# Cross-attention on one core: the first head's weights in two halves, xT behind pair 1's weights, and seven small warm-up matmuls on zeros from VectorE

## What is computed

```python
Q = (x @ Wq).reshape(B, -1, H, D).transpose(0, 2, 1, 3)
K = (ctx @ Wk).reshape(B, -1, H, D).transpose(0, 2, 1, 3)
V = (ctx @ Wv).reshape(B, -1, H, D).transpose(0, 2, 1, 3)
score = jnp.einsum('bhqd,bhkd->bhqk', Q, K) / math.sqrt(D)
attn = softmax(where(mask, score, -inf))
out = einsum('bhqk,bhkd->bqhd', attn, V).reshape(B, -1, H * D) @ Wo + x
return (out - mean) * rsqrt(var + 1e-5) * gamma + beta
```

## Time and profile before

| | |
|---|---|
| median of 3 runs | 318.01 us (317.92 to 318.31) |
| profiled execution, own time | 317.95 us |
| profiled execution, span from first to last instruction | 316.1 us |
| outside the span | 1.85 us |
| TensorE busy | 309.5 us (98%) |
| granted TensorE clock over the span | 0.997 |

### The profile page before, as it was taken

How to read it: one execution, slowest core, us unless ns; L and a number is a source line. 1 busy time by engine, 2 the same in 40 slices (tenths; PEclk the granted TensorE clock), 3 DMA queues, 4 the chain that set the end, 5 groups by cost and what they waited for, 6 DMA issues and landing times.

```text
span 316.1 us, 8051 instructions
## 1 busy us (share of the span) xinstructions
PE 309.5 (98%) x2584; PEld 303.4 (96%) x2584; DVE 253.1 (80%) x721; ACT 222.0 (70%) x601; POOL 181.3 (57%) x183
## 2 busy tenths in 40 slices
PE   8999999999999999999999999999999999999993
PEld 7998889999999999999999999999999999999992
DVE  0467778777999789987998889987998889975686
ACT  2446677768867787678777797678767887777640
POOL 1123476457864587558855586558755686457212
PEclk9999999999999999999999999999999999999998
DMA  7996443564354454384446535364355435440101
GB/s 254 358 400 242 137 150 117 158 218 134 98 163 160 159 175 140 141 239 142 133 126 208 172 133 163 129 214 156 113 187 185 170 100 184 143 155 4 35 0 66
DMA packets 46911, 50.27 MB, mean 159 GB/s; under 512 B 3504, under 2 KB 37040, under 8 KB 46896
## 3 DMA queue, kind: packets, MB, share of 16 engines
q1 hardware_dynamic: 46608, 49.56, 47.0%
q10 hardware_dynamic: 288, 0.52, 0.7%
HBM read 32.24 MB, written 17.83 MB: 158 GB/s over the span
## 4 chain that ended last, share of the span: by engine, by line
PE 95%; DMA 2%; DVE 1%; SPq 1%; POOLq 0%; issue 0%; POOL 0%
PE score_bank L321 25%; PE out_bank L321 19%; PE gL_bank L321 14%; PE tL_bank L321 13%; PE tU_bank L321 9%; PE gU_bank L321 7%; DMA wq_raw<-in_wqT 2%; PE spare_bank L321 1%; PE tL_bank L355 1%; PE spare_bank L355 1%; PE tL_bank L337 1%; PE tU_bank L337 1%; PE out_bank L361 1%; PE tU_bank L361 1%; PE out_bank L337 0%; PE spare_bank L337 0%
## 5 line engine op out<-in xcount | busy, mean ns | idle before, releaser
L1017 POOL TENSOR_TENSOR probs<-probs,inv_sum 128x512 f32<-128x512 f32 x64 | 66.7, 1043 | 84.4 <-DVE inv_sum L804 83.8
L615 ACT ACTIVATE probs<-neg_scores,neg_max 128x256 f32<-128x256 f32 x128 | 64.1, 502 | 36.1 <-DVE neg_max L793 36.0
L1040 POOL TENSOR_TENSOR pT_lo<-pT_raw,pT_hi 128x512 fp32r<-128x512 f32 x60 | 76.6, 1297 | 8.6 <-ACT pT_hi L572 8.6
L793 DVE CUSTOM_DVE_ANT_0 neg_scores<-score_bank,mask_bias 128x256 f32<-128x256 f32 x128 | 49.1, 420 | 6.3 <-PE score_bank L321 3.9
L814 DVE STREAM_TRANSPOSE squares<-probs 128x512 f32<-128x512 f32 x60 | 42.3, 706 | 1.0 <-DMA scratch<-squares 0.8
L572 ACT ACTIVATE tL_hi<-tL_bank 128x512 fp32r<-128x512 f32 x31 | 18.6, 599 | 29.6 <-PE tL_bank L321 29.6
L321 PE MATMUL score_bank<-ctxT_hi,gU 128*128 128x256 f32 x128 | 36.1, 282 | 0.0
L321 PE MATMUL score_bank<-ctxT_hi,gL_lo 128*128 128x256 f32 x128 | 35.9, 281 | 0.0
L321 PE MATMUL score_bank<-ctxT_lo,gU 128*128 128x256 f32 x128 | 35.9, 281 | 0.0
L321 PE MATMUL score_bank<-ctxT_lo,gL_hi 128*128 128x256 f32 x128 | 35.9, 280 | 0.0
L321 PE MATMUL score_bank<-ctxT_hi,gL_hi 128*128 128x256 f32 x128 | 35.6, 278 | 0.0
(11 more groups left out here) (167 smaller groups left out, 981.0 us busy)
## 6 DMA issues: line engine op xcount, KB each, us to landing
scratch<-squares SPq DMA_DIRECT2D x30, 512.0 KB, 2.8
pT_raw<-scratch SPq DMA_DIRECT2D x120, 128.0 KB, 3.1
xT_raw<-in_xT SPq DMA_DIRECT2D x8, 256.0 KB, 4.5
ctxT_raw<-in_ctxT SPq DMA_DIRECT2D x8, 256.0 KB, 4.7
wo_raw<-in_wo SPq DMA_DIRECT2D x4, 512.0 KB, 14.3
x_res<-in_x SPq DMA_DIRECT2D x8, 256.0 KB, 3.2
out<-y_out SPq DMA_DIRECT2D x7, 256.0 KB, 2.6
wq_raw<-in_wqT SPq DMA_DIRECT2D x3, 512.0 KB, 7.6
```

What stands on the lines that cost most here:

```text
L615: nc.scalar.activation(probs[j % 2][:, n, :], neg_scores[:, n, :], ACT.Exp, bias=neg_max[:, n:n + 1], scale=-1.0, accum_out=row_sum[:, n:n ...
L793: nc.vector.tensor_tensor_reduce(out=neg_scores[:, n, :], in0=score_bank[hh][:, q, :], in1=mask_bias[:], scale=-SCALE, scalar=3.0e38, op0= ...
L1017: nc.gpsimd.tensor_tensor(probs[j % 2][:, rows, :], probs[j % 2][:, rows, :], inv, ALU.mult) \
L1040: nc.gpsimd.tensor_tensor(pT_lo[j % 2][:, k].rearrange("p hh (q i r) -> p (hh q) i r", q=QT, i=ROWS), pT_raw[j % 2][:, k].rearrange("p i n ...
```

## The change

It has four parts. Head 0's wk and wq are loaded as one transfer per tile `d` instead of one per head, each with a semaphore of its own (`q_head_in[0]` and `[1]`; head 1 now has `q_head_in[2]`). `fold_A` runs `d` outside and `i` inside, for all heads, and waits for each `d` of head 0 apart. SyncE issues xT behind wk and wq of pair 1. The warm-up is 7 matmuls of 128 columns instead of 4 of 256, on zeros that VectorE sets (128x128) instead of GpSimd (128x256).

```diff
-WARMING = 4
+WARMING = 7
-        zeros = sb("zeros", [P, DI])
+        zeros = sb("zeros", [P, P])
-        q_head_in = [sem(f"q_head_in{h}") for h in range(2)]
+        q_head_in = [sem(f"q_head_in{n}") for n in range(DT + 1)]
@@ sync
-            for j in range(PAIRS):
-                if j > 0:
-                    tiles = slice(2 * j * DT, 2 * (j + 1) * DT)
-                    sp.dma_start(wk_raw[:, tiles], wkT[:, tiles]).then_inc(q_weights_in[j], 16)
-                    sp.dma_start(wq_raw[:, tiles], wqT[:, tiles]).then_inc(q_weights_in[j], 16)
-                else:
-                    for h in range(2):
-                        tiles = slice(h * DT, (h + 1) * DT)
-                        sp.dma_start(wk_raw[:, tiles], wkT[:, tiles]).then_inc(q_head_in[h], 16)
+            for d in range(DT):
+                sp.dma_start(wk_raw[:, d:d + 1], wkT[:, d:d + 1]).then_inc(q_head_in[d], 16)
+            sp.dma_start(wk_raw[:, DT:2 * DT], wkT[:, DT:2 * DT]).then_inc(q_head_in[DT], 16)
+            for j in range(1, PAIRS):
+                tiles = slice(2 * j * DT, 2 * (j + 1) * DT)
+                sp.dma_start(wk_raw[:, tiles], wkT[:, tiles]).then_inc(q_weights_in[j], 16)
+                sp.dma_start(wq_raw[:, tiles], wqT[:, tiles]).then_inc(q_weights_in[j], 16)
+                if j == 1:
                     load_xT(0)
@@ tensor, fold_A
-                if h < 2:
-                    pe.wait_ge(q_head_in[h], 32)
-                elif h % 2 == 0:
+                if h == 1:
+                    pe.wait_ge(q_head_in[DT], 32)
+                elif h > 0 and h % 2 == 0:
                     pe.wait_ge(q_weights_in[h // 2], 32)
-                for i in range(IT):
-                    for d in range(DT):
+                for d in range(DT):
+                    if h == 0:
+
+                        pe.wait_ge(q_head_in[d], 32)
+                    for i in range(IT):
                         ins = nc.tensor.matmul(dst[:, i * DL:(i + 1) * DL],
                                                wq_raw[:, h * DT + d, i * P:(i + 1) * P],
-                                               wk_raw[:, h * DT + d, :], start=d == 0, stop=d == DT - 1)
+                                               wk_raw[:, h * DT + d, :], start=d == 0 and i == 0, stop=d == DT - 1,
+                                               skip_group_check=True)
@@ tensor
-                nc.tensor.matmul(score_bank[0][:, 0, :], zeros[:, 0:P], zeros[:], start=True, stop=True)
+                nc.tensor.matmul(score_bank[0][:, 0, 0:P], zeros[:], zeros[:], start=True, stop=True)
@@ scalar
-            for h in range(2):
-                tiles = slice(h * DT, (h + 1) * DT)
-                act.dma_start(wq_raw[:, tiles], wqT[:, tiles]).then_inc(q_head_in[h], 16)
+            for d in range(DT):
+                act.dma_start(wq_raw[:, d:d + 1], wqT[:, d:d + 1]).then_inc(q_head_in[d], 16)
+            act.dma_start(wq_raw[:, DT:2 * DT], wqT[:, DT:2 * DT]).then_inc(q_head_in[DT], 16)
@@ vector
+            nc.vector.memset(zeros[:], 0.0).then_inc(zeros_made, 1)
@@ gpsimd
-            nc.gpsimd.memset(zeros[:], 0.0).then_inc(zeros_made, 1)
```

## The result

| | before | after |
|---|---|---|
| median of 7 runs each | 317.94 us (317.92 to 318.31) | 319.10 us (318.57 to 319.50) |
| profiled execution, own time | 317.95 us | 319.14 us |
| its span | 316.1 us | 317.3 us |

The ratio is 1.0032, 95% interval 1.0022 to 1.0041: slower by 0.7 to 1.3 us, outside the predicted range (317.4 to 318.4). So the sign holds both times and the size is between 0.3 and 1.3 us. The ratios compare all runs of two kernels and not their medians alone, so the two can differ by some tenths of a microsecond.

A forecast was written before the change was run, and what follows sets the result against it. The prediction took the landing of pair 1's weights at 9.07 us, then unbroken TensorE work, as the bound. Moving xT (-0.34 us) plus the halves' cost (+0.25) gave -0.09 on 317.95: 317.9 us, range 317.4 to 318.4.

The forecast's parts named there:

- What bounds the start: Kernel start: pair 1's weights landing at 9.07 us set it, and TensorE follows in one piece.
- Nothing behind absorbs a shift: After the start: TensorE is busy 98% of the span, so the end moves as much as the folds.
- xT behind pair 1: Start's load stream: pair 1 lands 0.65 us earlier, but a wait at head 4 limits the gain to 0.34 us.
- o: Start's load stream: total delay from splitting head 0's loads, taken as 0.25 us, bounds 0 and 1.34.
- The halves start TensorE earlier, which is worth nothing: Head 0: TensorE starts 0.7 us earlier, at 4.0 us, but then waits for pair 1 anyway; no gain.
- packet time: Head 0's loads: 256 more packets at 9 ns fixed time each, over 16 engines, cost 0.15 us.
- two more completions: Head 0's loads: two more transfers, each with 16 completion writes at 9 ns, cost 0.02 us.
- the ramp: Stream up to 2.5 us: if half-size packets take as long there, 0.085 us is lost.
- the 12.1 that I had named as a sign of being wrong: Pair 2's wq, expected at 11.4 to 11.8 us: landing after 12.1 would show the prediction wrong.
- Slower, by the halves in the stream: First 3 us: packet rate, not bytes, limits the loads; sum toward +1.0 us, 318.9 us; chance 0.08.
- Slower, by the clock: TensorE at the start: array stays longer at its lower clock level, head 4 0.5 us late, 318.5 us; chance 0.07.
- Small packets are free: Head 0's loads: splitting costs only 0 to 0.05 us, so -0.3 us, 317.6 us; chance 0.2.

The follow-up runs named there:

- e5: Changed kernel with head 0's first tile alone and the other three tiles of heads 0 and 1 in one transfer, on both queues: 317.86 us, ratio 1.0002.
- e8: Kernel before with xT issued behind pair 2 and its high part behind head 2's; whole transfers, old warm-up: 317.59 us, ratio 0.9987.
- e1: Kernel before with one edit, xT issued behind pair 1's weights: 317.83 us, ratio 0.9987.
- e15: The changed kernel, unaltered, run again: 318.57 us, ratio 1.0017.
- e9: Changed kernel with head 0's wq whole again on ScalarE; SyncE's wk stays in halves: 318.08 us, ratio 0.9996.
- e4: Changed kernel without the halves: whole transfers of head 0 and the old fold: 317.79 us, ratio 0.9989.
- e18: Changed kernel with the queues' tensors exchanged for heads 0 and 1: ScalarE issues head 0's wk in halves, SyncE wq whole: 318.01 us, ratio 0.9991.
- e16: Changed kernel with wq's second half and head 1 in one transfer on ScalarE; SyncE keeps wk's halves: 317.82 us, ratio 0.9988.
- e3: Kernel before with head 0 loaded and folded in halves; xT in front of pair 1 and old warm-up: 318.75 us, ratio 1.0014.
- e10: Changed kernel with head 0's wk whole again on SyncE; ScalarE's wq stays in halves: 319.40 us, ratio 1.0043.
- e17: Changed kernel with the queues' tensors exchanged for heads 0 and 1: SyncE issues head 0's wq in halves, ScalarE wk whole: 318.71 us, ratio 1.0024.
- e11: Kernel before (whole transfers, old warm-up) with xT issued by ScalarE as its third transfer: 318.15 us, ratio 1.0001.
- e12: Changed kernel with wq of head 1 issued on SyncE's queue instead of ScalarE's: 319.58 us, ratio 1.0044.
- e7: Changed kernel with head 1 loaded in halves as well: 318.94 us, ratio 1.0027.
- e13: Kernel before with xT behind pair 1, both queues waiting for head 0's landing before issuing more: 319.60 us, ratio 1.0042.
- e6: Kernel before with xT behind pair 1 and head 0's wk and wq each in two transfers of 64 partitions: 319.25 us, ratio 1.0041.

## Why the prediction was wrong, step by step

- **What bounds the start: right.** Landing of pair 1 and 2, and TensorE in one piece behind them. In the first profile head 5 came 1.25 us late and the time 1.19.
- **"Nothing behind absorbs a shift": right for a late start, not always for an early one.** At 41 us the store to `scratch` had 0.2 us of slack, and in four profiles with an early start it used that up; they lost 0.4 to 1.5 us behind the start (see e5). A busy share of 98% doesn't show such a limit.
- **xT behind pair 1: right.** Alone it gave pair 1 at 8.31 (8.42 predicted), the wait at head 4, and -0.4 us (-0.34 predicted, with o = 0). With xT behind pair 2 (e8) that wait is gone and head 5 starts 0.4 us earlier than in e1. The medians fell by another 0.2 us, but the ratio is the same as e1's, so this second gain isn't shown in the time.
- **The halves start TensorE earlier, which is worth nothing: right.** Head 0 started at 4.00 and its fold ended near 6.4 as predicted. But head 1, which I had done at 8.1, waited for its wk until 7.89.
- **What the halves cost: the step that failed.** I made o of three terms: packet time (0.15), two more completions (0.02), the ramp (0.085). Measured by pair 2's landing against 11.33, o is 1.6 us in the first profile, beyond the 12.1 that I had named as a sign of being wrong, and 0.7 us in e15, just short of it. It isn't a mis-sized term but one that was missing. The ramp, in which I looked for a loss, was no slower than before (227 against 84 GB/s). The packet time was about right too: in the changed kernel the 1 KB packets took 46 ns once the ramp was over, and 9 plus 36 ns per KB gives 46. The short transfers went fast, and then the stream fell into a trough of 165 to 313 GB/s that lasted 3 to 4 us, single packets stood still for up to 2 us, and the last part of each later transfer landed up to 1.8 us behind its first. I had priced what each packet costs in an even stream and its mean rate; I hadn't asked whether the stream stays even, though TensorE waits for its slowest part.
- **The rivals.** "Slower, by the halves in the stream" was the right side and the right place, with 0.08; its mechanism (the packet rate of the first 3 us) was not it. That its number, 318.9, lies near the measured one is luck. "Slower, by the clock" didn't happen: in the changed kernel the loads of head 1 were at the upper level, and in e1 even those of head 0 were (1.27 us for eight, at 4.73), without any gain, since TensorE then waited for pair 1. "Small packets are free" fails for wq and nearly holds for wk (by the medians e9 is 0.3 us above e4, e18 0.2).
- **The rule for the bytes of a packet**, that 512 B and more run at line rate ("DMA: Bandwidth & Descriptors" of the Trainium skill, Specifications), would have given 317.6. Packets of 0.46 KB on average did run fast, 350 in a microsecond in the earlier trace rows, and so did the halves themselves (350 GB/s from 2.5 to 3.0 us after the change); the loss was behind them. The Trainium skill's advice to join many small transfers into one large one ("DMA: Bandwidth & Descriptors", Rules for kernel authors) pointed the right way: e16 joins two and is rid of the loss.

**What is shown and what is open.** Shown by times: the halves bring the loss (e3, and e4 against the changed kernel); wq's halves bring it on either queue (e10, e17), and wk's bring 0.2 to 0.3 us by the medians on either (e9, e18), which is no more than the intervals are wide. Joining wq's second half to head 1's transfer removes it (e16; in e5 it is gone in the landings and the median, but not in the interval). A third whole transfer on ScalarE's queue doesn't matter (e11), nor on which queue wq of head 1 comes (e12), and more halves don't add to it (e7). Shown too: a stream that runs empty pays a ramp of 1.5 us (e13). Argued: that it takes the unevenness, and not the trough alone, to make the loss. For it, e16 has e15's trough without its unevenness and without the loss. Against it, e17 is slow by its times, while in its one profile pair 2's increments came within 0.90 us; and in e9, which is not slow, they took 1.31 us, as in e15, though the last came at 11.84 us, 0.2 earlier. Why packets stood still behind the halves, and why behind wq's more than wk's, is open. wq's rows lie 16 KB apart in memory and wk's 12 KB, and a half takes 1 KB of each row of wq and 768 B of wk; a layout with another pitch would test that, and wasn't tried.

## What to carry to other kernels

At the start of a kernel, with a stream of loads that everything waits for, reorder the transfers before you split them: moving xT back twice gave 0.6 us by the medians (0.1 to 0.7 by the interval), and splitting head 0's load lost about a microsecond. A split is priced by the last part to land of what comes behind it, not by how early its own first part lands, and not by the mean rate of the stream; if a first part must come early, leave one short transfer and join the rest to the next (e16). And an engine's wait, once covered, moves: look for the next transfer's slack (here 0.45 us at pair 2, and 0.2 us at a store 30 us later) before you count a whole gain. And look at single packets before you trust their mean.

## What the runs showed of the hardware that I had not expected

- The start of the stream varies between executions: from 2.0 to 2.5 us it moved 84 GB/s in the profile of before and 190 in e1, whose packets were as large. With 1 KB and 768 B packets it moved 227 in the changed kernel and 254 in e15, and lost more afterwards.
- DMA engines that ran empty needed 1.5 us to full rate again (58, 82, 188, 377 GB/s per half microsecond).
- Single packets can stand still: a 3 KB packet took up to 1.99 us in the changed kernel, beside some 0.12 us for most. From 3.5 to 7 us eight packets took over 0.5 us there and ten in e15, one in e1 and none before.
- The 16 increments of one 512 KB transfer came within 0.8 us before and within 1.8 us in the changed kernel, and the lag passed unchanged from pair 1 to pair 2.
- The rise of TensorE's clock moved between executions: head 0's eight loads took 2.42 us in the profile before and 1.27 us in e1, whose TensorE program differs in nothing.
- An issue behind or among those of 64 partitions took longer: 0.60 and 0.78 us for SyncE's two of 64 partitions in e6 and 0.60 for the next, of 128, where the same issue took 0.42 to 0.44 in the kernel before, in e1 and in the changed one. Whether the 64 partitions are the reason isn't shown.
